# MLP stage: two steps of the next first product moved ahead of the last down quarter, and small operations dealt anew between ScalarE, VectorE and GpSimd

## The reference

```
h2 = ln(x, g2, beta2)
x  = x + (gelu(h2 @ w1 + b1) @ w2 + b2)          # 256 -> 1024 -> 256
h  = h + x
xn = layernorm(h)
full_logits = xn @ gate_w.T                        # 8 experts + 1 shared
mult, sel = sparse_mixer(full_logits[:, :8])       # up to 4 experts per token
y_sh = (silu(xn @ sh_gate.T) * (xn @ sh_up.T)) @ sh_down.T
out  = h + w[shared] * y_sh + sum over chosen experts of w[e] * y_dyn[e]
```

## Time and profile before

| | us |
|---|---|
| median of 3 runs | 2683.14 (2682.89 to 2688.43) |
| the profiled execution | 2680.65 |
| its span, first to last instruction | 2678.9 |
| busy in the span: TensorE | 2370.8 (88%) |
| VectorE | 1851.4 (69%) |
| GpSimd | 1566.1 (58%) |
| ScalarE | 1533.9 (57%) |
| mean granted TensorE clock | 0.964 |

### The profile page before, as it was taken

How to read it: one execution, slowest core, us unless ns; L and a number is a source line. 1 busy time by engine, 2 the same in 40 slices (tenths; PEclk the granted TensorE clock), 3 DMA queues, 4 the chain that set the end, 5 groups by cost and what they waited for, 6 DMA issues and landing times. The chain is left out here.

```text
span 2678.9 us, 61218 instructions
## 1 busy us (share of the span) xinstructions
PE 2370.8 (88%) x22832; PEld 1728.2 (65%) x22832; DVE 1851.4 (69%) x4046; ACT 1533.9 (57%) x2859; POOL 1566.1 (58%) x1546
## 2 busy tenths in 40 slices
PE   3799999999999999999999957998998999995664
PEld 3588788888888888888888743444444444443553
DVE  3577777777777777777777742777877778775442
ACT  3566666666666666666666635555555655552232
POOL 1465656656565665656565532556656666666566
PEclk8999999999999999999999977999999999998888
DMA  4111111212111111111110020211211211100675
GB/s 150 44 62 62 43 60 62 66 37 66 62 41 62 41 41 41 45 37 41 42 40 26 14 82 25 70 48 60 80 52 57 79 49 41 46 21 16 151 138 71
DMA packets 115061, 152.21 MB, mean 57 GB/s; under 512 B 16537, under 2 KB 75917, under 8 KB 114768
## 3 DMA queue, kind: packets, MB, share of 16 engines
q1 hardware_dynamic: 88880, 124.46, 14.3%
q0 software_dynamic: 23808, 21.74, 4.6%
q10 hardware_dynamic: 2080, 2.10, 0.2%
HBM read 81.71 MB, written 90.96 MB: 64 GB/s over the span
## 5 line engine op out<-in xcount | busy, mean ns | idle before, releaser
L952 POOL TENSOR_TENSOR qkl<-fz,qkh 128x512 f16<-128x512 f32 x256 | 307.6, 1202 | 305.5 <-DVE qkh L849 305.5
L1817 POOL DMA_INDIRECT slot_dram<-xt,slot_u x256 | 258.5, 1010 | 74.5 <-issue 74.4
L521 PE MATMUL pF<-nh,qk_h 128*128 128x256 f16 x1024 | 281.2, 275 | 5.7 <-DVE nl L836 4.4
L523 PE MATMUL pF<-nl,qk_h 128*128 128x256 f16 x1024 | 280.6, 274 | 0.0
L522 PE MATMUL pF<-nh,qk_l 128*128 128x256 f16 x1024 | 280.6, 274 | 0.0
L964 POOL TENSOR_TENSOR ol<-on,oh 128x256 f16<-128x256 f32 x256 | 171.8, 671 | 153.3 <-ACT oh L786 153.3
L971 POOL TENSOR_TENSOR kvl<-kvacc,kvh 128x260 f16<-128x260 f32 x192 | 150.3, 783 | 108.1 <-ACT kvh L794 108.1
L763 ACT ACTIVATE sh<-sm 128x512 f16<-128x512 f32 x256 | 159.3, 622 | 84.9 <-DVE sm L872 84.9
L1797 POOL TENSOR_TENSOR al<-az,ah 128x512 f16<-128x512 f32 x64 | 78.9, 1232 | 204.3 <-DVE ah L1586 204.3
L740 ACT ACTIVATE rz<-pF 128x512 f32<-128x512 f32 x256 | 150.7, 589 | 81.9 <-PE pF L523 77.2
L846 DVE SCALAR_TENSOR_TENSOR fz<-pF,ez 128x512 f32<-128x512 f32 x256 | 175.3, 685 | 29.6 <-ACT ez L746 27.4
(11 more groups left out here) (313 smaller groups left out, 8565.7 us busy)
## 6 DMA issues: line engine op xcount, KB each, us to landing
xs<-in_x SPq DMA_DIRECT2D x128, 256.0 KB, 2.6
slot_dram<-blank SPq DMA_DIRECT2D x8, 1360.0 KB, 6.0
xg<-slot_dram SPq DMA_DIRECT2D x40, 272.0 KB, 3.2
h_dram<-hT SPq DMA_DIRECT2D x32, 256.0 KB, 2.1
x_dram<-x SPq DMA_DIRECT2D x32, 256.0 KB, 2.1
at_dram<-at SPq DMA_DIRECT2D x32, 256.0 KB, 2.2
x0b<-x_dram SPq DMA_DIRECT2D x16, 512.0 KB, 3.9
atb<-at_dram SPq DMA_DIRECT2D x16, 512.0 KB, 4.9
```

The source lines that it names most:

```text
L521: pe.matmul(out, wh, mh, start=first, stop=False, skip_group_check=True)
L523: return pe.matmul(out, wh, ml, start=False, stop=last, skip_group_check=True)
L952: nc.gpsimd.tensor_tensor(qkl[:, pair:pair + 2, cols], fz[:, n % 2, :, :], qkh[:, pair:pair + 2, cols], ALU.subtract).then_inc(fl_ready, 1)
L1817: nc.gpsimd.indirect_dma_start(io["slot_dram"], bass.IndirectOffsetOnAxis(slot_u[:, c, k:k + 1], 0), xt[:, i % 2, c, :], None, bounds_chec ...
```

## The change

1. `down(i-1)` is cut in two: quarters 0 to 2, then the new step `w1_ahead(i+1)`, then quarter 3. `w1_ahead` holds steps 0 and 1 of the first product of the next sequence, which stood at the head of the next body, ahead of `mean2`. Its wait for the banks pW is for az of quarter 2 and no longer of quarter 3.
2. The two casts xnh move from VectorE to ScalarE, each behind its xn.
3. The subtraction xnl of half 1 moves from GpSimd to VectorE. GpSimd keeps that of half 0.
4. The two copies of `turn_sums` (ht) move from ScalarE to VectorE, behind ob and the first two routing links.
5. Routing links 3 to 6 follow these copies, and each later group of three comes that much sooner; link 28 alone is left for `mask`.

```
                 if before:
-                    s["down"](i - 1)
+                    s["down"](i - 1, range(ST - 1))
+                if after:
+                    s["w1_ahead"](i + 1)
+                if before:
+                    s["down"](i - 1, (ST - 1,))
...
             def w1(i, before, js):
+                if js[0] > 0 or i == 0:
+                    product1(i, js)
+
+            def w1_ahead(i):
+                product1(i, (0, 1))
+
+            def product1(i, js):
...
                     if j >= 2:
                         pe.wait_ge(gz_ready, count(i, FT, j - 1))
-                    elif not (type(i) is int and i < 2):
-                        pe.wait_ge(az_ready, count(i, ST, -ST))
+                    elif i == 1:
+                        pe.wait_ge(gz_ready, FT)
+                    elif i >= 2:
+
+                        pe.wait_ge(az_ready, count(i, ST, -ST - 1))
...
-            def down(i):
+            def down(i, ks):
...
-                for k in range(ST):
+                for k in ks:
...
-                mm.then_inc(down_done, 1)
+                if ks[-1] == ST - 1:
+                    mm.then_inc(down_done, 1)
...
                 nc.scalar.activation(rs3[:, :], ln3[:, :], ACT.Exp, scale=-0.5).then_inc(rs3_step, 1)
+                for m in range(DT):
+                    act.wait_ge(xn_ready, count(i, DT, m + 1))
+                    nc.scalar.activation(xnh[:, m, :], xn[:, m, :], ACT.Copy).then_inc(xnh_ready, 1)
...
-            def turn_sums(i):
-                for half in range(2):
-                    act.wait_ge(ht_done, count(i, 2, half + 1))
-                    if not at_start(i):
-                        act.wait_ge(ob_ready, count(i, CH, 0))
-                    nc.scalar.activation(ht[:, 2 * half:2 * half + 2, :],
-                                         pA[half][:, :].rearrange("p (c n) -> p c n", c=2), ACT.Copy).then_inc(ht_ready, 1)
...
-                        routing(i - 1, EXP1_AFTER + 3 * j, EXP1_AFTER + 3 * j + 3)
+                        routing(i - 1, min(FIRST_LINKS + 3 * j, LAST_LINK), min(FIRST_LINKS + 3 * j + 3, LAST_LINK))
...
-                for m in range(DT):
-                    ve.wait_ge(xn_ready, count(i, DT, m + 1))
-                    nc.vector.tensor_copy(xnh[:, m, :], xn[:, m, :]).then_inc(xnh_ready, 1)
-
-            def down(i):
+                ve.wait_ge(xnh_ready, count(i, DT, DT))
+                nc.vector.tensor_tensor(xnl[:, 1, :], xn[:, 1, :], xnh[:, 1, :], ALU.subtract).then_inc(xnl_ready, 1)
+
+            def turn_sums(i):
+                for half in range(2):
+                    ve.wait_ge(ht_done, count(i, 2, half + 1))
+                    if not at_start(i):
+                        ve.wait_ge(ob_ready, count(i, CH, 0))
+                    nc.vector.tensor_copy(ht[:, 2 * half:2 * half + 2, :],
+                                          pA[half][:, :].rearrange("p (c n) -> p c n", c=2)).then_inc(ht_ready, 1)
+                routing(i, EXP1_AFTER, FIRST_LINKS)
...
-                for m in range(DT):
-                    gp.wait_ge(xnh_ready, count(i, DT, m + 1))
-                    nc.gpsimd.tensor_tensor(xnl[:, m, :], xn[:, m, :], xnh[:, m, :], ALU.subtract).then_inc(xnl_ready, 1)
+                gp.wait_ge(xnh_ready, count(i, DT, 1))
+                nc.gpsimd.tensor_tensor(xnl[:, 0, :], xn[:, 0, :], xnh[:, 0, :], ALU.subtract).then_inc(xnl_ready, 1)
...
+FIRST_LINKS = 6
+LAST_LINK = 27
```

More of the change, by code:

```diff
@@ L1208, in run @@
             s["gate_up"](SEQS - 1, None, range(ST))
-            s["down"](SEQS - 1)
+            s["down"](SEQS - 1, range(ST))
         def at_start(i):
@@ L1406, in _ @@
                          rstd3=nothing, logits=logits, turn_rows=turn_rows, turn_sums=turn_sums,
-                         counts=counts))
+                         counts=counts, w1_ahead=w1_ahead))
         @block.scalar
@@ L1512, in _ @@
             run(act, dict(mean2=mean2, centre2=centre2, var2=var2, scale2=nothing, shift2=shift2, mask=nothing, w1=w1, w2=nothing, mean3=mean3, gate_up=gate_up, var3=nothing,
-                          rstd3=rstd3, down=nothing, logits=logits, turn_rows=turn_rows, turn_sums=turn_sums,
-                          counts=counts))
+                          rstd3=rstd3, down=nothing, logits=logits, turn_rows=turn_rows, turn_sums=nothing,
+                          counts=counts, w1_ahead=nothing))
             act.wait_ge(ew.w_in[0], 16)
@@ L1598, in rstd3, with down @@
                     nc.vector.tensor_tensor(xn[:, m, :], xc3[:, m, :], rs3[:, :], ALU.mult).then_inc(xn_ready, 1)
-                for m in range(DT):
-                    ve.wait_ge(xn_ready, count(i, DT, m + 1))
-                    nc.vector.tensor_copy(xnh[:, m, :], xn[:, m, :]).then_inc(xnh_ready, 1)
-            def down(i):
+                ve.wait_ge(xnh_ready, count(i, DT, DT))
[8 more added lines that the diff above has]
+                routing(i, EXP1_AFTER, FIRST_LINKS)
+            def down(i, ks):
+                if ks[-1] < ST - 1:
+                    return
                 ve.wait_ge(routed, count(i, 1, 1))
@@ L1748, in mask @@
             def mask(i):
-                routing(i, EXP1_AFTER + (0 if type(i) is int and i == SEQS - 1 else 3 * FT), MASK_AFTER)
+                routing(i, FIRST_LINKS if i == SEQS - 1 else LAST_LINK, MASK_AFTER)
             def counts(i):
@@ L1758, in _ @@
             run(ve, dict(mean2=nothing, centre2=centre2, var2=nothing, scale2=scale2, shift2=shift2, mask=mask, w1=w1, w2=w2, mean3=mean3, gate_up=gate_up, var3=nothing,
-                         rstd3=rstd3, down=down, logits=logits, turn_rows=nothing, turn_sums=nothing, counts=counts))
+                         rstd3=rstd3, down=down, logits=logits, turn_rows=nothing, turn_sums=turn_sums, counts=counts,
+                         w1_ahead=nothing))
             ve.wait_ge(ew.wh_ready, 1)
@@ L1858, in _ @@
             run(gp, dict(mean2=mean2, centre2=nothing, var2=var2, scale2=nothing, shift2=nothing, mask=nothing, w1=w1, w2=w2, mean3=mean3, gate_up=gate_up, var3=nothing,
-                         rstd3=rstd3, down=down, logits=nothing, turn_rows=nothing, turn_sums=nothing, counts=counts))
+                         rstd3=rstd3, down=down, logits=nothing, turn_rows=nothing, turn_sums=nothing, counts=counts,
+                         w1_ahead=nothing))
             gp.wait_ge(rows_sent, 16 * CH * TOP * SEQS)
```

## The result

| | before | after |
|---|---|---|
| median of 10 runs each, us | 2684.33 (2678.88 to 2688.69) | 2670.01 (2662.90 to 2678.45) |
| ratio after / before | | 0.9947, 95% interval 0.9931 to 0.9963 |
| the profiled execution, us | 2680.65 | 2674.46 |
| its span, us | 2678.9 | 2672.4 |
| mean granted TensorE clock | 0.964 | 0.958 |

A forecast was written before the change was run, and what follows sets the result against it. TensorE's queue was taken to set body length. Gains of 19.4 (bodies 1 to 13), 5.2 (mask), 2.1 (body 0), 1.5 (body 14) and 1.5 (after body 15), 29.7 us, gave 2651 profiled, 2653 as median; range 2646 to 2667.

The forecast's parts named there:

- Two steps ahead of the last quarter: Seam: 2.59 us of matmuls moved ahead remove 1.08 us of waiting for al; the quarter ends at 2020.74.
- The casts and the low half: Seam: xnl ready at 2020.2, bounds 2019.8 to 2021.2, so the row transposes start 0.48 us earlier.
- Rival 2: Seam: VectorE's low half waits for a GpSimd x1 sum, the seam gives 1.0 not 1.49; 2660 us, chance 0.17.
- The turned sums on VectorE: Behind the transposes: ht copies leave ScalarE, fifth step starts 1.49 us earlier; new wait of some 1.3 us ahead of mean2.
- Rival 1: Ahead of mean2: VectorE copies of up to 1.2 us decide, fifth step gains 0.64 not 1.49; 2664 us, chance 0.13.
- The routing links: VectorE: four links move ahead of the first gz wait, mask ready at 2043.0, counts start 2.02 us earlier.
- Rival 3: VectorE's six moved operations are held up by GpSimd's sends, some 5 us lost per body; 2748 us, chance 0.03.
- The body: MLP stage: body to body 49.0 to 49.6 us instead of 51.05; 1.49 us gained in each of bodies 1 to 13.
- the mask's 0.4: Ahead of the counts: TensorE's wait for VectorE's mask goes in 9 bodies, 5.2 us in all with the overhang.
- The step that failed: Whole forecast: room upward in stalls and stretches of lower clock, which may fall elsewhere; no size given.
- the two ends of the stage: Body 14 gains ScalarE's 1.5 us; after body 15 GpSimd's chain of sends begins 1.5 us earlier.

The follow-up runs named there:

- edit 1 alone: The kernel before with only the two first-product steps moved ahead of the last down quarter; one run, 2690.74 us against a median before of 2687.99.
- the second execution: The changed kernel run and profiled again with no edit; 2669.03 us, ratio 0.9936 to the kernel before.
- the fill: The changed kernel plus six 512-column matmuls, result unused, where TensorE waited for ht ahead of mean2; 2654.86 us, ratio 0.990 to the kernel before.
- edit 4 undone: The changed kernel with the ht copies put back on ScalarE; one run, 2670.86 us against 2689.61 for the kernel before.
- the split: The changed kernel with step 0 alone ahead of the last quarter and step 1 behind the transposes of the sums; 2655.34 us, ratio 0.9887 to the kernel before.

## Why the prediction was right in its steps and wrong in its sum

**Two steps ahead of the last quarter**: right. No wait for al is left, and the transposes start 0.11 us behind the start of the quarter's last matmul. Alone it gains nothing (edit 1 alone), as the argument had it: the gain comes through ScalarE's chain.

**The casts and the low half**: right, on the good side. VectorE's half, expected at about 1.1 us with up to 1.66, and the copies of the turned sums, in VectorE's timeline of the changed kernel at the seam of the earlier trace rows, with the copies' group behind it (min/median/max ns):

```profile
2015.30 0.87 DVE L1610 TENSOR_TENSOR xnl<-xn,xnh 128x512 f16<-128x512 f32 x1 [0.70 <-ACT xnh L1493]
2017.33 1.66 DVE L1630 SCALAR_TENSOR_TENSOR ob<-pY,w,ht 128x256 f32<-128x256 f32 x4 [1.16 <-PE pY L1253]
2020.24 1.29 DVE L1617 COPY ht<-pA 128x512 f32<-128x512 f32 x2
2021.45 0.41 DVE L1672 TENSOR_TENSOR pair<-lg 128x256 f32<-128x256 f32 x1
...
L1617 DVE COPY ht<-pA x32: 679/686/692, 1671.5 to 2422.9; 128x512 f32<-128x512 f32 x32
```

It took 0.87 us, 1.15 at the most, and GpSimd's one half 1.60 where 1.2 had been taken. VectorE's half was ready at 2016.17, 0.85 us ahead of the transposes at 2017.02. Rival 2 is out.

**The turned sums on VectorE**: right. 0.69 us were taken for a copy, and it is 0.686, at most 0.692. Rival 1 is out. The wait ahead of mean2 was put at 1.2 to 1.3 and is 1.36.

**The routing links**: right. The counts wait for no mask, and the link at 2021.45 runs in 0.41 us. Rival 3 is out.

**The body**: 51.05 less 1.49 and less the mask's 0.4 is 49.1 to 49.2; measured 49.15. For bodies 0 to 13 the prediction has 19.4 + 5.2 + 2.1 = 26.7 us, the traces 26.6 + 1.0.

**The step that failed** is the one sentence that carried no number: "It has room upward in stalls and stretches of lower clock, which may fall elsewhere." The sum puts the lower clock at nothing, without a reason: it takes TensorE's clock at the seam as it was in the trace of before. The sequence and mean2's duration were there for a bound, and the trace of before has the lower clock in the seams of bodies 9, 10, 12 and 14. The edits put the logits' 24 matmuls of nine columns, the transposes of the sums and a wait of 1.3 us directly ahead of mean2, and mean2 is four fp32 matmuls that take some 1.7 us at full clock. At half the clock they take another 1.7; in 13 bodies that bounds the loss at 22 us. The same edits take away each wait that could have swallowed it. Measured: 1.45 us in 6 of 14 bodies, 8.7 us, and in the second execution 11.5 in 7. With a term of half the bound, 11 us, the forecast would have been 2664.

The lower clock fell at two more places. Behind the wait in body 8 it costs 1.6 us and in body 14 2.7, so in the first execution of the changed kernel it costs 13.0 us in the stage, against 0.9 in bodies 9, 10 and 12 before.

Two smaller terms failed too. The stall in GpSimd's sends was seen as a thing that falls anywhere; it falls in the same body each time, and its length differs between executions of one kernel (3.30 and 4.71 us before, 5.65 and 5.47 after). That body 8 costs 6.3 us instead of 2.65 is this length and the lower clock behind the wait: before, the stall of 4.71 us cost 5.6. That the change made the stall dearer is not shown. And the two ends of the stage, -1.5 us each in the sum, came out as +0.65 and +1.45. In body 14 the steps moved ahead leave TensorE with nothing between the transposes and gz; with the fill the body takes 44.64 us against 46.74 before, -2.1, so the chain was right there as well and the clock ate it. Behind body 15 GpSimd stood 4.79 us in its sends where it had stood 4.11, which is 0.7 of the 1.45; the rest is open.

By the medians the forecast missed by 17 us, and the two traces account for it: 10.7 for what disturbs the bodies, 5.1 for the two ends and 1.9 in the routed stage, less 0.9 that the undisturbed bodies gave beyond the forecast. Of these some 12 are the lower clock.

Open: why one seam falls and its neighbour, alike to 0.01 us, doesn't; what makes GpSimd stand at these two sends; and why the lower clock lasts longer at the ends of the attention stage in one execution than in the next.

## What to carry to other kernels

When waits are taken off TensorE's path, price the clock with them: as a bound, multiply what runs directly behind the new seam by two (mean2: 1.80 to 3.40 us here), and ask which wait used to hide that. A new wait can be filled with a step of real work (the split, 0.9887), and if there is none even useless matmuls pay, here 14 us (0.990); the two can't be told apart by their times. Of two kernels, compare the same body over more than one execution before a longer body is put down to the change: body 8 of the kernel before took 53.70 and 56.65 us. And follow the next wait to the queue behind it: the step from 0.9892 to 0.9839 was two sends that stood ahead of a small subtraction on GpSimd.

## What the runs showed of the hardware that was not expected

- The clock falls at seams that are alike. The changed kernel lost it in 6 and in 7 of 14 bodies, in two executions, with four bodies in common. In all 14 seams mean2 follows 24 small matmuls, eight transposes and a wait of about 1.3 us. With six matmuls in the wait, 1.3 us, or six of the first product, the profiled executions have no slow mean2.
- The same slow mean2 costs nothing where waits behind it are longer than the loss (edit 1 alone, ten seams), 0.35 to 0.45 us with edit 4 undone, and 1.45 in the changed kernel.
- GpSimd stands 3.3 to 5.7 us ahead of its 114th and its 227th send of the stage, in all 13 profiles. The 114th starts between 2058 and 2089 us, so it isn't the time alone that decides. The distance of 113 points to a count, but in all 13 these are the same two sends of the program, and nothing else was tried.
- A VectorE subtraction out of SBUF gets its turn among GpSimd's: it took 0.87 us between GpSimd's own half (1.60 us instead of 1.2) and the two x1 sums, which went from 2.49 to 2.94 us. By the Trainium skill, SBUF — State Buffer, section "SBUF: two separate sides", one of such a pair blocks for the whole instruction of the other. The trace agrees that both pay. A copy out of PSUM, with one operand, kept to 679 to 692 ns in 32 of 32.
